# The last chunk's three maxima in another order, the FFN's rows turned behind an output product, and a layer's last normalisation moved into the FFN stage

## What is computed

```python
x = x + _L0_attn_ref(_layernorm(x), Wq, bq, ...)        # retention, 16 heads
x = x + _L0_xattn_ref(_layernorm(x), ctx_512, ...)      # cross-attention, 16 heads
x = x + _L0_ffn_ref(_layernorm(x), w1, w2, w3)
...
    scores = jnp.einsum('bhsr,bhlr->bhsl', q_r, k_r)    # 1600 query rows by 1444 keys per batch
    attn = jax.nn.softmax(scores, axis=-1)
    ctx_c = jnp.einsum('bhsl,bld->bhsd', attn, kv_r)
...
    x1 = _bitlinear(x, w1)
    x2 = _bitlinear(x, w2)
    hidden = jax.nn.sigmoid(x1) * x2
    return _bitlinear(hidden, w3)                       # weights rounded to -1, 0, 1; 704 hidden
```

## Time and profile before

| | |
|---|---|
| median of 3 runs | 2365.67 us (2363.03 to 2366.86) |
| the profiled execution, its own time | 2365.12 us |
| its span, first to last instruction | 2363.3 us |
| outside the span | 1.8 us |
| PE busy | 2220.1 us, 94% |
| POOL busy | 1829.2 us, 77% |
| DVE busy | 1688.6 us, 71% |
| ACT busy | 1197.9 us, 51% |
| mean granted clock of TensorE | 0.964 |

### The profile page before, as it was taken

One profiled execution on the slowest core, in us unless ns is written; L12 is line 12 of the kernel. 1 busy time (PEld: TensorE's weight loads), 2 busy tenths in 40 slices (PEclk: granted clock), 3 DMA queues, 4 the chain that ended last, 5 costly groups with the idle time before them and its releaser, 6 DMA issues. The chain is left out here.

```text
span 2363.3 us, 47265 instructions
## 1 busy us (share of the span) xinstructions
PE 2220.1 (94%) x15390; PEld 1416.5 (60%) x15390; DVE 1688.6 (71%) x2771; ACT 1197.9 (51%) x1933; POOL 1829.2 (77%) x818
## 2 busy tenths in 40 slices
PE   7989858999996999999999999999999999999798
PEld 4545446777772555555555555555555555555587
DVE  6888847888875667667667667667667767767775
ACT  4323222222222666666666666666666666665243
POOL 3554527988983799999999999999999999989211
PEclk9889978999996999999999999999999999999999
DMA  4000024666676344324334333333333432431011
GB/s 143 22 15 28 15 73 138 191 180 187 190 195 152 79 93 99 96 65 98 87 74 96 81 82 89 84 87 81 83 95 74 89 96 67 96 90 39 22 47 41
DMA packets 239505, 216.16 MB, mean 91 GB/s; under 512 B 124500, under 2 KB 213768, under 8 KB 239304
## 3 DMA queue, kind: packets, MB, share of 16 engines
q1 hardware_dynamic: 239432, 215.22, 35.8%
HBM read 129.68 MB, written 60.78 MB: 81 GB/s over the span
## 5 line engine op out<-in xcount | busy, mean ns | idle before, releaser
L1768 POOL TENSOR_TENSOR x_acc<-x_acc,x_prob 128x1600 f32<-128x1600 f32 x315 | 1138.7, 3615 | 26.0 <-ACT x_prob L1798 2.1
L1798 ACT ACTIVATE x_prob<-x_scores 128x800 f32<-128x800 f32 (+1 forms) x768 | 605.6, 838 | 70.5 <-PE x_scores L2118 60.7
L2151 PE MATMUL x_context<-x_prob,x_kv 128*64 128x400 f32 x2816 | 550.5, 512 | 7.0 <-ACT x_ctxs L1838 6.7
L1910 DVE TENSOR_REDUCE x_mx<-x_ring 115x2 f32<-115x1024 f32 x310 | 380.1, 1226 | 50.7 <-PE x_ring L2218 30.9
L1919 DVE TENSOR_REDUCE x_mx<-x_ring 115x1 f32<-115x466 f32 (+3 forms) x352 | 221.8, 630 | 240.3 <-PE x_ring L2225 240.0
L1818 ACT COPY x_half<-x_ring 115x466 f32<-115x466 f32 (+3 forms) x352 | 190.0, 540 | 312.9 <-PE x_ring L2225 312.8
L2151 PEld LDWEIGHTS x_context<-x_prob,x_kv 128*64 128x64 f32 x2816 | 171.3, 136 | 241.5 <-issue 232.5
L2118 PE MATMUL x_scores<-x_qh,x_dh 64*128 64x400 f32 (+1 forms) x1536 | 272.4, 349 | 0.3 <-ACT x_prob L1798 0.3
L2118 PE MATMUL x_scores<-x_ql,x_dh 64*128 64x400 f32 (+1 forms) x1536 | 267.1, 341 | 0.0
L2118 PE MATMUL x_scores<-x_qh,x_dl 64*128 64x400 f32 (+1 forms) x1536 | 267.0, 342 | 0.0
L1923 DVE TENSOR_REDUCE x_mx<-x_half 115x1 f32<-115x466 f32 (+3 forms) x352 | 220.2, 626 | 4.4 <-ACT x_half L1818 1.4
(11 more groups left out here) (206 smaller groups left out, 3637.0 us busy)
## 6 DMA issues: line engine op xcount, KB each, us to landing
scratch_qh<-q_qsh SPq DMA_DIRECT2D x64, 200.0 KB, 3.2
scratch_ql<-q_qsl SPq DMA_DIRECT2D x64, 200.0 KB, 3.5
x_qm<-scratch_qh SPq DMA_DIRECT2D x64, 200.0 KB, 3.6
x_qh<-scratch_qh SPq DMA_DIRECT2D x64, 200.0 KB, 3.3
x_ql<-scratch_ql SPq DMA_DIRECT2D x64, 200.0 KB, 3.7
x_rden<-scratch_rden SPq DMA_DIRECT2D x64, 200.0 KB, 3.5
scratch_kr<-q_krot SPq DMA_DIRECT2D x32, 384.0 KB, 2.3
x_kr<-scratch_kr SPq DMA_DIRECT2D x32, 384.0 KB, 4.6
```

The source lines that it names most:

```text
L1768: pool.tensor_tensor(acc[0:rows, parity], first, prob[0:rows, c % PR], ALU.add).then_inc(acc_done.sem, 1)
L1798: act.activation(prob[0:rows, c % PR, u * HALF:(u + 1) * HALF].rearrange("p (j s) -> p j s", j=2), psc[0:rows, u, :, 0:BANK], ACT.Exp).the ...
L1910: dve.tensor_reduce(best[0:block_rows(r), :, r, i], src[0:block_rows(r), :, 0:b - a], AX.X, ALU.max).then_inc(read_sem(u), 1)
L2151: mm = pe.matmul(pav[DC * s:DC * s + DC, j, 0:BANK], kv[0:rows, parity, c], prob[0:rows, c % PR, cols], start=c == 0, stop=c == LC - 2)
```

## The change

The list `order` of cross-attention has, in chunk 11, the pair ahead of the scores and the wide unit behind them, as in the other chunks. ACT copies the second half of that pair ahead of both exponentials of chunk 11, where it did so between them. DVE's `negm` waits for the wide unit alone. In the FFN stage PE turns the next group's rows behind output product m - 1 = 2. The second group's rows are normalised by DVE as its first work in the FFN stage, and no longer ahead of the barrier. SP no longer waits for the last two stores ahead of the barrier, but ahead of the load of the FFN's last group. The tile `x2` and its semaphores belong to an object that both stages share.

```diff
@@ the list of units
-            r, i = next(narrow) if c > 0 else (None, None)
-            pair = [("half", r, i, 0), ("half", r, i, 1)] * (c > 0)
-            own += pair if c < LC - 1 else [next(wide)]
+            if c > 0:
+                r, i = next(narrow)
+                own += [("half", r, i, 0), ("half", r, i, 1)]
             own += [("scores", 0), ("scores", 1)]
             if c == 2:
                 own += [("den",), ("turn", 2)]
-            elif 0 < c < LC - 1:
+            elif c > 0:
                 own.append(next(wide))
-            elif c == LC - 1:
-                own += pair
             own.append(("context",))
@@ SP, end of cross-attention
             store_x2(B - 1, 1)
-            for parity in range(2):
-                sp.wait_ge(x2_stored.sems[parity], x2_stored.done(B - 2 + parity, parity))
@@ ACT
                 for c in range(LC):
-                    if c < LC - 1:
-                        copy_halves(n, c)
+                    copy_halves(n, c)
...
                         for u in range(2):
-                            if c == LC - 1 and u == 1:
-                                copy_halves(n, c)
                             exponentials(n, c, u)
-                    elif c == LC - 1:
-                        copy_halves(n, c)
@@ DVE
                             wait_read(dve, n, last_max)
-                            wait_read(dve, n, (*copied[-1][:3], 0))
-                            dve.wait_ge(half_read.sem, half_read.at(n, len(copied)))
                             dve.tensor_reduce(negm[:], mx[:], AX.X, ALU.max, negate=True).then_inc(max_ready.sem, 1)
...
             output(B + 1, 1)
-            normalise_second()
@@ FFN, SP
                 sp.wait_ge(x_kept.sem, x_kept.at(k - 2, 1))
+                if is_at(k, NG - 1):
+                    for last in range(2):
+                        sp.wait_ge(f.x2_stored.sems[last], f.x2_stored.done(B - 2 + last, last))
@@ FFN, DVE
                 for m in range(FC):
+                    if m == 0 and is_first(k):
+                        normalise(k + 1, 1 - parity)
                     gate(k, m)
@@ FFN, PE
                     hidden(k, parity, m)
+                    if 1 <= m <= GB and not is_first(k):
+                        output(k - 1, 1 - parity, m - 1)
                     if m == 3 and more:
                         turn_xn(k + 1)
-                    if 1 <= m <= GB and not is_first(k):
-                        output(k - 1, 1 - parity, m - 1)
```

More of the change, by code:

```diff
@@ L1485, in phase_cross_attention @@
         xr = sb("xr", [S, 2, E])
-        x2 = sb("x2", [S, 2, E])
         psc = ps("scores", [P, 2, 2, 512])
@@ L1557, in phase_cross_attention @@
         m_loaded = transfer("m_loaded", 32)
-        x2_stored = transfer("x2_stored", 16, 32)
+        x2, x2_stored = f.x2, f.x2_stored
         dh_copied = sig("step_high_copied", 3, 5)
@@ L2018, in second_rows @@
                 dve.tensor_scalar(f.veps[:], f.mv[:, :, 1], EPS, None, ALU.add).then_inc(f.row_veps.sem, 1)
[L2020 to L2025, removed]
             def split_rows():
@@ L2342, in __init__ @@
         self.xl = sb("xl", [P, 2, EC, GT], F32R)
+        self.x2 = sb("x2", [S, 2, E])
+        self.x2_stored = Transfer(ctx, nc, "x_x2_stored", 32)
         self.loaded = sig("weights_loaded", 0)
```

## The result

| | before, same chip | changed |
|---|---|---|
| median | 2365.36 us (2363.03 to 2366.86, 4 runs) | 2342.49 us (2341.68 to 2345.15, 4 runs) |
| ratio, 95% interval | | 0.9908 [0.9893, 0.9924] |
| profiled execution, its span | 2365.12, 2363.3 | 2345.15, 2343.4 |

The two profiled executions are 19.9 us apart in span.

A forecast was written before the change was run, and what follows sets the result against it. PE was taken to set the slot period, and one chain the FFN stage. Gains of 16.3 (chunk 11) and 1.4 (barrier) less 2.0 (turning) gave 15.7 us, time 2349.6 us, range 2346 to 2358.5.

The forecast's parts named there:

- The start-up slot: Start-up slot of cross-attention: with the pair first, DVE can reduce while the wide unit waits, for some 0.8 us.
- the barrier: Barrier between the stages: without normalise_second and SP's wait for the stores, PE starts the FFN stage 1.4 us earlier.
- the turning: FFN groups k = 1 to 6: output product 2 waits for DVE's add, losing 0.33 us a group, 2.0 us.
- the slot term: Chunk 11 of cross-attention: mT starts 0.50 us earlier a slot, 15.5 us over 31 slots.
- The bound that I wrote down: Chunk 11's upper bound: not more than both of PE's waits with the lost issue, 0.66 us a slot, 20.5 us.
- The second case: Behind the barrier: rival that the clock stays high, up to 1.55 us more, time 2348.3 us; chance 0.20.
- The cover of the moved normalisation: Start of the FFN stage: DVE's idle 3.98 us before its first gate covers the moved normalisation (1.38 us), costing nothing.
- The thin cover of the output product: Behind mT and turn 0: POOL's first ctxn comes early enough for the output product, cover falling from 0.8 to 0.3 us.
- One sign of failure: Cross-attention slot: the prediction fails if the output product waits for ctxn.
- half the gain: Cross-attention slots: rival that POOL or another engine takes back half, leaving 0.25 us a slot, time 2357.6; chance 0.13.
- no shorter slots: Cross-attention slots: rival that POOL's sums set the period, leaving small terms, +0.6 us, time 2366; chance 0.09.
- the late copy: Chunk 11: rival that ACT's copy delays the wide unit, 0.63 us a slot lost, time 2385; chance 0.06 with similar losses.

The follow-up runs named there:

- The repeat: The changed kernel itself, unaltered, measured once more against the kernel before on the next experiments' chip: 2345.17 us against 2363.54, ratio 0.9916.

## Why the prediction was right, and where it was wrong

The mechanism was right in each part, and three terms were near. The start-up slot gave 0.78 (0.8 predicted); the barrier opened 1.42 earlier relative to `rstd` (1.4); the turning lost 0.37 a group (0.33). Over six groups that is 2.2 us, which the kernels with the turning alone and with it put back show; between the two profiles of the result the stretch lost 1.95 (2.0 predicted), since 0.27 us of it came back behind the last turning, for a reason that is open. The kernel with the add moved shows that DVE's order is the cause of the loss. As said, PE waits nowhere behind chunk 11's scores.

**The step that failed** is the size of the slot term: 0.50 us predicted, 0.59 measured, over 31 slots 18.3 and not 15.5 us. I had the wide reduce start 0.53 us behind the start of its matmuls, a distance read in the old order, and put DVE's own end second: 1.87 behind the pair, against 1.95 for PE. The trace has the wide unit 1.40 behind the pair (1.42 predicted), its fill ready 0.47 later at most, and the reduce at 1.87, where DVE came free. From there all links have the predicted lengths, up to mT at 3.39 and not 3.46. That makes 0.57 in chunk 11, so this start holds 0.07 of the missing 0.09; the last 0.02 a slot, 0.6 us in all, is open. The bound that I wrote down, 0.66 a slot, held; the range did not use it. With it, and with the clock case added (20.5 + 0.8 + 1.4 - 2.0 + 1.55 = 22.2 us), the range would have begun at about 2343, and the first median, 2342.49, would still lie just below it.

**The clock.** The second case came true beside the first in the profiled run: the full 1.00 behind the barrier. The windows from 1 to 2 us behind the start of the first FFN block (columns as in the earlier trace rows), in the changed kernel, in the kernel with the turning alone (gap 3.28), in the one with the barrier alone (gap 1.92) and in the last one above, with the load of `w3` moved (gap 1.92):

```profile
2201.54:2202.54 1.00, 1.00 (x7) 0.98 (x6) 1.00 (x2) 0.26 (x1) 0.69 (x1) 1.00 0.00 0
```

```profile
2218.22:2219.22 1.00, 1.00 (x7) 0.99 (x6) 0.00 (x0) 0.28 (x1) 0.69 (x1) 1.00 0.00 0
```

```profile
2223.02:2224.02 1.00, 1.00 (x5) 0.97 (x4) 1.00 (x2) 0.09 (x1) 0.69 (x1) 0.66 0.00 0
```

```profile
2198.83:2199.83 1.00, 1.00 (x5) 0.95 (x4) 0.00 (x0) 0.05 (x1) 0.69 (x1) 0.64 0.00 0
```

Of ten traces with the short gap (1.77 to 1.95 us) three have fallen towards the low level there; of four with the long gap (3.28 to 3.35) one stays high. The short gap goes with the high clock, but does not make sure of it. The Trainium skill, page "TensorE: Matmul & The Clock Gate", section "Why this matters for your kernels", says that long idle gaps drop the clock and short ones do not; at the barrier these traces agree in most cases and break it both ways, and the gap of 2.54 us in the last group was followed by the low clock in ten of 14. What decides stays open. The high clock gave 0.93 us here, less than 1.55. In the kernel with the turning alone, whose normalisation is not moved, it gave 1.39; and with the normalisation behind the gate 0.33 of the difference came back. So the larger part of the shortfall is the gate that waits for the normalisation.

**The cover of the moved normalisation** was said to cost nothing, and cost 0.3 us. It stood beside POOL's copy of 1.89 us, and the first of its four instructions, begun 0.11 us behind the copy, took 1.93 us instead of 0.40 and ended 0.15 behind the copy's end. The Trainium skill, page "SBUF — State Buffer", section "Who interferes with whom", says that VectorE in some modes and GpSimd share a pair of ports, and that the one that comes second is blocked for the other's whole instruction. This case's trace agrees, with its 1.93 us; the prediction left out what POOL does at that point.

**The thin cover of the output product.** One sign of failure that the prediction named did appear. In 27 slots the loading of the product's weights (PEld) now waits for `ctxn` by name, for 0.20 us, as here behind the mT shown above:

```profile
1518.61 1.54 PEld L2188 LDWEIGHTS x_ring<-x_wco,x_ctxn 128*100 128x100 f32 x8 [0.20 <-POOL x_ctxn L1745]
```

It cost nothing in the loop: with `ctxn` 3.7 us earlier the product starts at the same distance from mT. The cover failed in slot 30, where no keys are turned: 0.58 us back. This explains why the stretch from the last mT to the FFN stage is 0.88 us shorter and not 1.4.

**The rest of the miss.** From profile to profile the gain was 20.0 us and not 15.7: the slots gave 2.8 more, the clock 0.9, the stages ahead of cross-attention, in which nothing differs, 1.0, and slot 30 took 0.5. The first median lies another 2.7 us below its own profiled run. The repeat, with 18.4 us by medians, shows that this is how far such runs spread. Of the rivals, half the gain and no shorter slots fell by the period of 44.2 us; the late copy exists as a mechanism, near the size I gave it (0.55 a slot lost, 0.63 predicted), and the changed kernel avoids it.

All four versions with the add ahead of the normalisation have lower ratios to the kernel before than the changed kernel (0.9908 and 0.9916): 0.9878 with the add alone, then 0.9897, 0.989 and 0.9883. Only the interval of the first lies clear of that of the changed kernel on the same chip; the other three were measured on another. The four intervals overlap, so which is best stays open.

## What to carry to other kernels

Where two engines hand banks to each other, put the work that needs a copy by a third engine first, beside something long, and check where that third engine takes the copy: here its place alone turned 0.59 us a slot gained into 0.55 lost. When a start is the later of two nearly equal times, 0.08 us apart, take both as open, and let the range carry the difference times the number of slots. Before an instruction is moved on one engine, look at what stands ahead of the result that the next engine really needs: moving PE's turning cost 0.37 us a group, and moving DVE's add with it gained 1.30 over that.

## What the runs showed of the hardware

POOL's copy of 1.89 us stretches what DVE does beside it, and not at the barrier alone. In seven of the eight groups one of DVE's subtractions `f_hl` meets it, and takes 1.07 to 1.27 us where the median is 0.57. The instructions of that line (count, ns min/median/max), and DVE and POOL at one of the seven places:

```profile
L2505 DVE TENSOR_TENSOR f_hl<-f_hid,f_hh x48: 559/568/1274, 2205.4 to 2330.6; 118x400 fp32r<-118x400 f32 x40, 114x400 fp32r<-114x400 f32 x8
```

```profile
2235.50 1.89 POOL L2433 TENSOR_TENSOR f_y<-f_x,f_ones 100x1024 f32<-100x1024 f32 x1
2236.55 1.27 DVE L2505 TENSOR_TENSOR f_hl<-f_hid,f_hh 118x400 fp32r<-118x400 f32 x1
```

What moving this copy would give was not tried.

A gap of some 1.9 us at the barrier was followed by the full clock in seven traces and by a fall towards half of it in three; the gap of 2.54 us in the last group by the full clock in four and by half of it in ten, which cost the changed kernel 1.5 us. One large load ahead of small round trips on SP's queue made a slot 1 to 6 us longer, by another amount in each run.
